# Cell passes of a graph network: schedule words one group ahead, two sum buffers, and one-hots of 128 lanes for a last block

## What is computed

```python
h = maximum(layernorm(x), 0); x = x + gin(h, edge_attr_64, src, dst)    # features pass
h = maximum(layernorm(x), 0); x = x + edge_mlp(h, src, dst, edge_attr_8) # mlp pass
h = maximum(layernorm(x), 0); x = x + sage(sage(h))                      # two cell passes
h = maximum(layernorm(x), 0); x = x + gcn(h)                             # one cell pass

def sage(x):
    agg = segment_sum(x[src], dst, num_segments=n)
    return x @ W_self + (agg / maximum(deg, 1)[:, None]) @ W_neigh + b
```

## Time and profile before

| what | us |
|---|---|
| three runs | 8915.97, 8932.15, 8933.47; median 8932.15 |
| the profiled execution's own time | 8954.18 |
| its span in the trace | 8952.5, mean granted clock 0.729 |
| busy: TensorE, VectorE, ScalarE, GpSimd | 4891.5, 5244.9, 1976.7, 3365.2 |
| the three cell passes, first reduce to last | 5797.9 to 6743.7, 6853.2 to 7800.3, 7960.1 to 8906.1 |

### The profile page before, as it was taken

How to read it: one execution, slowest core, us unless ns; L and a number is a source line. 1 busy time by engine, 2 the same in 40 slices (tenths; PEclk the granted TensorE clock), 3 DMA queues, 4 the chain that set the end, 5 groups by cost and what they waited for, 6 DMA issues and landing times. The chain is left out here.

```text
span 8952.5 us, 265733 instructions
## 1 busy us (share of the span) xinstructions
PE 4891.5 (55%) x94327; PEld 3979.6 (44%) x94328; DVE 5244.9 (59%) x16996; ACT 1976.7 (22%) x3084; POOL 3365.2 (38%) x3400
## 2 busy tenths in 40 slices
PE   1222222224444454444466667588776877768775
PEld 1222222222344444444455555455555555545554
DVE  4434433435544554454577777667775677666776
ACT  1111111112211111111100000254323532235322
POOL 5777777772477777777500000010000000000000
PEclk8555555556666666666677777699987999869998
DMA  3222222220233333333222222211101110011101
GB/s 86 59 57 60 59 59 58 60 58 19 79 89 89 89 92 89 89 89 89 59 65 79 81 77 85 94 50 38 28 23 50 46 34 28 30 66 46 34 28 42
DMA packets 277911, 548.41 MB, mean 61 GB/s; under 512 B 81684, under 2 KB 106900, under 8 KB 274825
## 3 DMA queue, kind: packets, MB, share of 16 engines
q1 hardware_dynamic: 143124, 411.34, 14.8%
q0 software_dynamic: 107552, 114.03, 6.6%
q10 hardware_dynamic: 26656, 16.06, 0.6%
HBM read 468.81 MB, written 72.33 MB: 60 GB/s over the span
## 5 line engine op out<-in xcount | busy, mean ns | idle before, releaser
L554 POOL DMA_INDIRECT store<-table,store x3136 | 3141.3, 1002 | 1038.4 <-issue 955.1
L707 PE MATMUL ps_all<-store 128*128 128x65 bf16 (+1 forms) x18816 | 991.3, 232 | 1709.7 <-DVE store L626 1550.2
L1204 PE MATMUL ps_all<-store 128*128 128x192 bf16 x13416 | 1564.1, 261 | 514.2 <-DVEq L1294 280.9
L707 PEld LDWEIGHTS ps_all<-store 128*128 128x128 bf16 x18816 | 944.5, 124 | 1760.8 <-issue 1760.8
L1285 DVE TENSOR_SCALAR store<-lanes,turned 128x256 bf16<-128x256 bf16 x8346 | 1669.7, 280 | 50.4 <-DVE turned L1281 42.3
L1204 PEld LDWEIGHTS ps_all<-store 128*128 128x128 bf16 x13416 | 1120.8, 102 | 866.1 <-issue 826.5
L1260 ACT CAST store<-ps_all 128x768 bf16<-128x768 f32 x1350 | 1076.3, 798 | 1747.6 <-PE ps_all L1339 1701.4
L1232 POOL DMA_INDIRECT store<-table_b,spill_row x225 | 216.1, 960 | 2442.4 <-PE ps_all L1339 2287.2
L729 PE MATMUL ps_all<-wide,store 128*128 x9408 | 508.7, 235 | 813.5 <-DVE store L642 813.5
L729 PEld LDWEIGHTS ps_all<-wide,store 128*128 128x128 bf16 x9408 | 478.3, 126 | 839.1 <-issue 838.6
L682 DVE TENSOR_TENSOR store<-store 128x512 f32<-128x512 f32 x196 | 135.6, 692 | 1101.2 <-DMA store<-table,store 1101.2
(11 more groups left out here) (228 smaller groups left out, 5459.3 us busy)
## 6 DMA issues: line engine op xcount, KB each, us to landing
store<-in_dst_rows SPq DMA_DIRECT2D x196, 512.0 KB
store<-lows_d SPq DMA_DIRECT2D x75, 784.0 KB, 5.2
store<-in_edge_attr SPq DMA_DIRECT2D x196, 256.0 KB, 2.6
store<-table,store POOLq DMA_INDIRECT x3136, 2.5
store<-cells_d SPq DMA_DIRECT2D x114, 392.0 KB, 3.0
turned<-cells_d SPq DMA_DIRECT2D x111, 392.0 KB
cells_d<-store SPq DMA_DIRECT2D x75, 392.0 KB, 5.7
wide<-attr_d SPq DMA_DIRECT2D x588, 48.0 KB
```

The costliest lines, as they stand in the source:

```text
L554: nc.gpsimd.indirect_dma_start(rows_f[:, g % SLOTS, j, :], None, table, bass.IndirectOffsetOnAxis(ap=src[:, g * TILES + j:g * TILES + j + ...
L707: last = nc.tensor.matmul(ps_pair[r % 2][:, b * width:(b + 1) * width], onehot[r % 2][b][:, j, :], value[r][:, j, i, 0:width], start=(b == ...
L1204: last = nc.tensor.matmul(to, hot[:, q, half * P:(half + 1) * P], rows[:, q, :] if q < SLOT_TILES else spill, start=(q == 0), stop=True, s ...
```

## The change

- The 12-register load at the top of an iteration goes. Each body now reads six words, its next group's four and the lowest and end block of the group behind that: on VectorE behind the first build, on TensorE behind the sixth of the seven chunks (function following).
- reduce_visit and add_visit take a buffer number: first and third visits use sums[0], second and fourth sums[1]. The wait ahead of a reduce is for the add before the last one where the buffers alternate.
- The signal to TensorE is given by the reduce itself, and VectorE waits on the same semaphore before the add. s_read and the sem_inc of L1294 are gone.
- build has a branch: if more than one block is left (w + 1 < stop) the 26 one-hots have 256 lanes as before, otherwise 128.

The diff, without the list of semaphore names and the renaming of sums in past_pass:

```diff
@@ -1151,7 +1151,8 @@
                       for _ in range(2)]
             place = [turned[:, 1, CELL_ROW + k * SLOTS_OF:CELL_ROW + (k + 1) * SLOTS_OF] for k in range(3)]
             assert at[0] <= ARENA, at
-            sums = turned[:, 0, 0:P]
+            rest_sums = turned[:, 0, 0:P]
+            sums = [rest_sums[:, k * D:(k + 1) * D] for k in range(2)]
             rest_ones, rest_diag = turned[:, 0, P:2 * P], turned[:, 0, 2 * P:3 * P]
             rest_hot = turned[:, 0, 3 * P:3 * P + P // 2].bitcast(BF16)
             rest_rows = turned[:, 0, 4 * P:4 * P + PARTS * D // 2].bitcast(BF16)
...
@@ -1163,32 +1164,42 @@
             ps_spread, ps_rest = ps_all[:, 0:P], ps_all[:, 512:512 + PARTS * D]
             n_pick = -(-SLOT_TILES // PICK)
 
-            def schedule(eng, it, n):
-
-                regs = [eng.alloc_register(f"cell_word_{nc.next_id()}") for _ in range(n * SCHED)]
-                eng.load(regs, sched[0:1, bass.ds(it * (CELL_STEP * SCHED), n * SCHED)])
-                return [ranged(eng, regs[k:k + SCHED]) for k in range(0, n * SCHED, SCHED)]
-
-            def ranged(eng, regs):
+            def ranged(eng, regs, donate=True):
 
                 most = CELLS * (WINDOWS + 1)
-                return (eng.snap(regs[0], donate=True, min_val=0, max_val=WINDOWS - 1),
-                        eng.snap(regs[1], donate=True, min_val=1, max_val=WINDOWS),
-                        eng.snap(regs[2], donate=True, min_val=1 - WINDOWS, max_val=most),
-                        eng.snap(regs[3], donate=True, min_val=1 - WINDOWS, max_val=most))
+                return (eng.snap(regs[0], donate=donate, min_val=0, max_val=WINDOWS - 1),
+                        eng.snap(regs[1], donate=donate, min_val=1, max_val=WINDOWS),
+                        eng.snap(regs[2], donate=donate, min_val=1 - WINDOWS, max_val=most),
+                        eng.snap(regs[3], donate=donate, min_val=1 - WINDOWS, max_val=most))
 
             def over_rounds(eng, body):
 
                 rounds = CELLS // CELL_STEP
-                of = schedule(eng, 0, 1)
-                body(-1, CELL_STEP - 1, [None] * CELL_STEP + of)
+                regs = [eng.alloc_register(f"cell_word_{nc.next_id()}") for _ in range(SCHED + 2)]
+
+                def behind():
+
+                    return (eng.snap(regs[SCHED], min_val=0, max_val=WINDOWS - 1),
+                            eng.snap(regs[SCHED + 1], min_val=1, max_val=WINDOWS))
+
+                def words():
+
+                    low, end, more, pairs = ranged(eng, regs[0:SCHED], False)
+                    return low, end, more, pairs, *behind()
+
+                def following(it, r):
+                    def load():
+                        eng.load(regs, sched[0:1, bass.ds(it * (CELL_STEP * SCHED) + (r + 1) * SCHED, SCHED + 2)])
+                    return load
+
+                eng.load(regs[SCHED:SCHED + 2], sched[0:1, 0:2])
+                body(-1, CELL_STEP - 1, [None] * SCHED + list(behind()),
+                     following(-1, CELL_STEP - 1))
                 with nc.Fori(0, rounds, engines=[eng.engine], hint_back_edge=True) as it:
-                    of = schedule(eng, it, CELL_STEP + 1)
                     for r in range(CELL_STEP):
-                        body(it, r, of)
-                of = schedule(eng, rounds, CELLS - rounds * CELL_STEP)
+                        body(it, r, words(), following(it, r))
                 for r in range(CELLS - rounds * CELL_STEP):
-                    body(rounds, r, of)
+                    body(rounds, r, words(), following(rounds, r))
 
             def there(it, r, k):
                 return within(it, r, k, CELL_STEP)
...
@@ -1206,14 +1217,14 @@
                                             start=(q == 0), stop=True, skip_group_check=True)
                 return last
 
-            def reduce_visit(of):
-
-                return nc.vector.tensor_reduce(sums[:, 0:D], of.rearrange("p (i d) -> p d i", i=PARTS), AX.X, ALU.add)
-
-            def add_visit(w):
+            def reduce_visit(of, k):
+
+                return nc.vector.tensor_reduce(sums[k], of.rearrange("p (i d) -> p d i", i=PARTS), AX.X, ALU.add)
+
+            def add_visit(w, k):
 
                 to = agg[:, bass.ds(w, 1), 0:D].rearrange("p o d -> p (o d)")
-                return nc.vector.tensor_tensor(to, sums[:, 0:D], to, ALU.add)
+                return nc.vector.tensor_tensor(to, sums[k], to, ALU.add)
 
             with nc.Block() as block:
                 @block.gpsimd
...
@@ -1276,51 +1287,56 @@
                         nc.vector.memset(agg[:, WINDOWS:PAIR_END, :], 0.0)
                         nc.vector.tensor_copy(agg[:, 0:WINDOWS, 0:D], start[:, :, :]).then_inc(s_add, 1)
 
-                    def build(k, g, w, placed, n_placed, signal):
+                    def build(k, g, w, stop, placed, n_placed, signal):
 
                         nc.vector.tensor_scalar(place[k], slot_dst[:, bass.ds(g * SLOTS_OF, SLOTS_OF)], first[:, bass.ds(w, 1)],
                                                 1.0, ALU.subtract, ALU.subtract).then_inc(placed, 2)
                         reach(dve, placed, n_placed)
+                        with dve.If(w + 1 < stop):
+                            compare(k, 2 * P).then_inc(signal, 2)
+                        with dve.Else():
+                            compare(k, P).then_inc(signal, 2)
+
+                    def compare(k, n):
                         for q in range(SLOTS_OF):
-                            last = nc.vector.tensor_scalar(pairs_hot[k][:, q, :], lanes[:, :], place[k][:, q:q + 1], None,
+                            last = nc.vector.tensor_scalar(pairs_hot[k][:, q, 0:n], lanes[:, 0:n], place[k][:, q:q + 1], None,
                                                            ALU.is_equal)
-                        last.then_inc(signal, 2)
-
-                    def add_up(of, w, n_before, signal):
-
-                        reach(dve, s_add, n_before + 1)
-                        reduce_visit(of).then_inc(s_read, 1)
-                        reach(dve, s_read, n_before + 1)
-                        dve.sem_inc(signal, 1)
-                        add_visit(w).then_inc(s_add, 1)
-
-                    def body(it, r, of):
+                        return last
+
+                    def add_up(of, w, k, added, signal, count):
+
+                        reach(dve, s_add, added)
+                        reduce_visit(of, k).then_inc(signal, 1)
+                        reach(dve, signal, count)
+                        add_visit(w, k).then_inc(s_add, 1)
+
+                    def body(it, r, words, following):
                         g0 = it * CELL_STEP
                         g = g0 + r
+                        low, end, more, pairs, low1, end1 = words
                         if there(it, r, 0):
-                            low, end, more, pairs = of[r]
                             with dve.If(low + 2 < end):
-                                build(2, g, low + 2, s_place_more, pairs + (low + 2), s_hot_more)
+                                build(2, g, low + 2, end, s_place_more, pairs + (low + 2), s_hot_more)
                         if there(it, r, 1):
                             k = (r + 1) % 2
-                            low1 = of[r + 1][0]
-                            build(k, g0 + (r + 1), low1, s_place, g0 * 2 + (2 * r + 4), s_hot)
+                            build(k, g0 + (r + 1), low1, end1, s_place, g0 * 2 + (2 * r + 4), s_hot)
+                            following()
                         if not there(it, r, 0):
                             return
                         hold(dve, s_sum, g0 + (r + 1))
-                        add_up(ps_first[r % 2], low, (more + low) + g, s_done)
+                        add_up(ps_first[r % 2], low, 0, (more + low) + (g0 + (r + 1)), s_done, g0 + (r + 3))
                         with dve.If(low + 1 < end):
                             reach(dve, s_sum_more, more + (low + 1))
-                            add_up(ps_extra[0], low + 1, (more + low) + (g0 + (r + 1)), s_add_more)
+                            add_up(ps_extra[0], low + 1, 1, (more + low) + (g0 + (r + 1)), s_add_more, more + (low + 3))
                         with dve.If(low + 2 < end):
                             with dve.Fori(low + 2, end, 2) as w:
                                 reach(dve, s_sum_more, more + w)
-                                add_up(ps_extra[1], w, (more + w) + g, s_add_more)
+                                add_up(ps_extra[1], w, 0, (more + w) + g, s_add_more, more + (w + 2))
                                 with dve.If(w + 1 < end):
                                     reach(dve, s_sum_more, more + (w + 1))
-                                    add_up(ps_extra[0], w + 1, (more + w) + (g0 + (r + 1)), s_add_more)
+                                    add_up(ps_extra[0], w + 1, 1, (more + w) + (g0 + (r + 1)), s_add_more, more + (w + 3))
                                 with dve.If(w + 2 < end):
```

(8 more changed lines are left out.)

8 lines of the change are left out of this document (4 added, 4 removed).

## The result

| | before | changed |
|---|---|---|
| median of 16 runs, us | 8928.93 | 8944.59 |
| lowest, highest | 8913.91, 8937.62 | 8927.12, 8956.15 |
| profiled execution: time, span | 8954.18, 8952.5 | 8944.36, 8942.6 |

The ratio is 1.0019, with an interval of 1.0011 to 1.0026: 16 us slower, at the edge of what can be told from no change. The forecast was 8802, 130 us faster. The changed time lies inside the stated range, which held both signs, but the forecast itself missed the sign.

What follows compares the result with a forecast made beforehand. The prediction took VectorE, largely its instruction stream, to set the pace. Its terms summed to -177 us, -156 after TensorE's share, about -130 with code size: 8824 from 8954.18, then 22 lower for the median, 8802; range 8730 to 9130.

Steps and rivals of the forecast that it cites:

- (e): VectorE's cell loop grows from 314 to 494 instructions; hint assumed to work, 27 us added, between 0 and 162.
- The reading of the mlp rows: Edge-pass loops: 338 instructions turn in 3.6 us, cell loops of 314 in 0.2, so the limit lies between.
- TensorE's share: First 29 groups of a pass, where TensorE ends last: 7 us a pass taken off, turning -177 into -156.
- the bound of -109: Lower bound on the saving, in us, if 87 of 225 groups gain nothing at all.
- (a): VectorE's load leaves the loop top, hidden behind 26 queued one-hots: 95 us saved, 13 back for register copies.
- (b): Sum buffers around reduce and add: dropped signal saves 52 us, moved register pair 31, second buffer itself nothing.
- (c): Branch in a build, between place vector and first one-hot: 0.22 us wide, 0.42 narrow, 96 us added.
- (d): Narrow one-hots in 126 builds: 33 ns less each, 108 us saved, bounds 79 and 229.
- rival 2: A larger saving from the narrow one-hots than forecast; its size isn't in the text given; chance 0.07.
- The forecast's -156: Launch total in us over the three cell passes, after TensorE's share and before the code-size cost.
- -130: Launch total in us: -156 with 27 added for code size, against the profiled execution's 8954.18.
- the 27 that had been set aside: Code-size cost of forward jumps in VectorE's cell loop: 45 x 0.6 us, an estimate between 0 and 162.

Runs made afterwards that it cites:

- e10: e7 without the prefetch hint on the loop's back edge; ratio 1.0071 to the kernel before.
- e1: The changed kernel with VectorE's cell loop placed at slot 0 of a fetch block in all three passes; ratio 0.9921 to the kernel before.
- e4: The changed kernel, but TensorE reads 8 registers for two groups at its loop's top; ratio 0.9982 to the kernel before.
- e6: The kernel before with only VectorE's load moved behind the build, TensorE reading 8 words at its loop's top; 8856.94 us, ratio 0.9922.
- e7: The changed kernel with VectorE's loop at slot 0 and TensorE's 8 words read at its loop's top; 8772.06 us, ratio 0.9829 to the kernel before.
- e9: e7 with VectorE's loop at slot 16, 20 and 40 in the three passes; ratio 0.9956 to the kernel before.
- e2: The changed kernel with VectorE's cell loop placed at slot 64 of a fetch block in all three passes; ratio 1.0246 to the kernel before.

## Why the prediction was wrong

- **(e), the step that failed.** The text saw that 494 instructions are beyond what the mlp loop showed, and then took the hint to solve it in every pass, pricing only 27 us of forward jumps. In two passes the back edge did stay at 0.3 us; in the third it took 2.3, and the pass cost 75 us against the kernel before and 101 to 107 against the other two passes. The step missed that the question isn't the length alone but the length and where it begins, which nothing in the change sets. At a start that fits the hint keeps the loop in place (e10), and it doesn't save one that doesn't fit: 2.3 us a turn with it at slot 40 or 64, 3.1 without it at slot 0. Where the loops of the changed kernel begin in its three passes isn't known; that only the third doesn't fit is read from its turns and packets, and from e1, which mends it by the place alone. So that two passes met the forecast was luck.
- **The reading of the mlp rows.** That a limit lies between 314 and 338 instructions was wrong for a loop with a hint. Those two loops differ in the hint too; with it, 494 stay (e1).
- **TensorE's share.** The sum took 7 us a pass off for TensorE in the early groups, half of its new load. On VectorE 13 us a pass were then left to gain there, and 6 and 2 were lost in the first two passes. Two values were off: the load of 6 registers is 0.82 us and not 0.48, since the line through 4 and 12 registers doesn't hold between them; and most of it shows as a gap, 0.50 us in each group. Moving it back gave 16 us a pass (e4), some 9 of it idle time and 7 matmuls at a higher clock, a term that the sum didn't have. The earlier trace rows had shown TensorE last in these groups, and the bound of -109 for all parts together was the better value: the first two passes gained 26 and 33 us, 3 x 29 = 88 for the launch.
- **(a)**, on VectorE: 12 to 16 us a pass in the late groups for 18 expected (e6). Right in kind, about a quarter too high. The cover for the load is there: when VectorE's queue goes on to the branch behind the 26 one-hots, 11 of them have still to start (in 320 of 321 builds of the changed kernel), which is 1.8 us at 0.163 each and 2.2 at 0.197.
- **(b)**: 69 us for the launch against 83; 22 us a pass against 21 in the late groups. That the second buffer itself is worth nothing wasn't tried apart from the signal.
- **(c)**: right. Between place vector and one-hots VectorE waits 47.6 us a pass (e7: 48.2), 16.4 before: 31 more, and 32 were the forecast.
- **(d)**: right. The 33 ns were the author's choice between the 24 and the 70 of the earlier trace rows, and 128 lanes took 34 less than 256. The larger saving of rival 2, with 0.07 in the chances, is shown by no run: the narrow one-hots stand 0.163 us apart, the wide ones 0.197.
- **The totals.** The forecast's -156 are 52 us a pass, by visits and builds about 39 in the late groups and 13 in the early ones. Against -130: third pass +104, early groups about 3 x 17 = +51 (4 us lost for 13 gained), late groups about 3 x 3 = +10 (36 us a pass for 39), and the 27 that had been set aside, -27. That is +138, of the 146 that were missed. With both defects mended the changed kernel reaches 8772, 157 below, with 38 us a pass in the late groups and 10 to 12 in the early ones: what the sum without (e) had said. The early part of that agreement is helped by TensorE's shorter load at the loop's top, which the change did not have.

## What to carry to other kernels

Doubling a body by a branch adds code as well as a branch: count the loop's instructions, registers and compares included, and look for the instruction queue's packets and the time of the loop's turn, pass by pass, since the same loop can stay in one place and be fetched anew in another. A sum near zero over three equal stages is a reason to look at each alone. And what is moved off one engine's critical place need not be moved on the other: place a load per engine, by which of them comes last in each stage, and read the registers in fours, as long as a trace shows what it shows here (8 in 0.59 us, 6 in 0.82).

## What the runs showed of the hardware

- A VectorE loop of 494 instructions stays in place from slot 0, 16 or 20 (e1, e7, e9), with 6 to 10 packets over a pass, and is fetched anew from slot 40 or 64 (e9, e2), with 185 to 190. The turn is 0.27 to 0.29 us in the one case and 2.3 in the other.
- Without the hint the same loop at slot 0 (e10) turns in 3.1 us, with 175 to 184 packets a pass.
- A miss isn't only at the turn: in e2 the compares other than the loop's are followed by 59 us a pass more than in e1; in e10, without the hint, by none more than in e9. And in the changed kernel's third pass 28 builds waited 44 us between place vector and one-hots, 21 of them in the step from a register instruction to the semaphore wait right behind it (1.3 us for 0.2), where no jump stands.
- A load of 1 register takes 0.31 us, of 4 0.34, of 8 0.59, of 12 0.85, but of 2 0.55 and of 6 0.82: those left over from a multiple of four cost about 0.24 each. (1 register from three loads of TensorE behind the passes, 2 from two loads of VectorE at their start; the third of those took 1.75.)
- An instruction of 26 that writes 128 lanes in place of 256 starts 0.163 us after the last one instead of 0.197, read from the 4.31 and 5.18 us of 26.
